# Gated alignment, memory, attention and expert layers on one core: inputs laid out ahead, row jumps scanned once per five steps, key parts split beside the scan and kept in eight places

## The reference

```python
x = x + jnp.tanh(g_xattn[0]) * _L0_xattn_ref(ctx_1024, _layernorm(x, axis=-1))
x = x + jnp.tanh(g_ffn[0]) * _L0_ffn_ref(_layernorm(x, axis=-1), ...)
x = x + jnp.tanh(g_xattn[1]) * _L1_xattn_ref(_layernorm(x, axis=-1), ctx_1024, ctx_1024, ...)
x = x + jnp.tanh(g_ffn[1]) * _L1_ffn_ref(_layernorm(x, axis=-1), ...)

# _L0_xattn_ref, for each batch: small = context (1500), large = x (56)
D = sqrt(max(aa + bb - 2.0 * small @ large.T, 0.0))
R[i, j] = D[i, j] + min(R[i-1, j], R[i, j-1], R[i-1, j-1])
# backtrack from the last corner; of equal ones the diagonal, then i - 1
expanded = zeros((56, 128)).at[j_idx].add(small[i_idx])
# _L1_xattn_ref: 16 heads of 8, keys and values from the context
scores = einsum('bhqd,bhkd->bhqk', Q, K) / sqrt(8)
ctx = einsum('bhqk,bhkd->bhqd', softmax(scores), V)
```

## Time and profile before

| quantity | value |
|---|---|
| device time, median of 3 runs | 730.74 us (726.15 to 734.12) |
| span of the profiled execution | 751.1 us |
| that execution against the median | 20.4 us longer |
| PE, DVE, ACT, POOL busy | 445.6, 444.4, 292.7, 202.9 us |
| data moved | 53.37 MB |

### The profile page before, as it was taken

One profiled execution on the slowest core, in us unless ns is written; L12 is line 12 of the kernel. 1 busy time (PEld: TensorE's weight loads), 2 busy tenths in 40 slices (PEclk: granted clock), 3 DMA queues, 4 the chain that ended last, 5 costly groups with the idle time before them and its releaser, 6 DMA issues.

```text
span 751.1 us, 10182 instructions
## 1 busy us (share of the span) xinstructions
PE 445.6 (59%) x3881; PEld 308.9 (41%) x3881; DVE 444.4 (59%) x1078; ACT 292.7 (39%) x486; POOL 202.9 (27%) x218
## 2 busy tenths in 40 slices
PE   4798211133105787965274105894695695996996
PEld 3798211121003556934172002563463463663443
DVE  5855999998914765455047407783574574815122
ACT  4553332334553457411052000461452452673443
POOL 1221354546253662067706300010101101110000
PEclk9755555556655556986576555896987987996999
DMA  6542000040152431023307999064946857600000
GB/s 164 153 120 72 0 1 0 27 138 33 45 144 86 131 104 62 2 18 95 95 2 92 115 144 120 10 72 54 117 63 71 101 70 79 226 3 1 0 0 14
DMA packets 57825, 53.37 MB, mean 71 GB/s; under 512 B 9456, under 2 KB 48304, under 8 KB 57648
## 3 DMA queue, kind: packets, MB, share of 16 engines
q1 hardware_dynamic: 43152, 39.83, 32.5%
q10 hardware_dynamic: 13088, 9.22, 3.9%
q0 software_dynamic: 1536, 3.67, 1.6%
...
## 4 chain that ended last, share of the span: by engine, by line
PE 39%; DVE 15%; issue 8%; DMA 5%; another core or an unknown queue 3%; ACT 3%; SPq 3%; POOL 1%; ACTq 0%; DVEq 0%; POOLq 0%
PE banks L1568 7%; PE banks L1592 7%; PE banks L1615 5%; PE banks L1471 4%; DVE work L1318 4%; PE banks L1657 3%; PE banks L1665 3%; DMA query_parts<-work 3%; PE banks L1529 3%; DVE mx L1090 2%; SPq L417 2%; DVE arena L1308 2%; PE banks L1432 2%; DMA arena<-query_parts 1%
## 5 line engine op out<-in xcount | busy, mean ns | idle before, releaser
L1090 DVE TENSOR_REDUCE mx<-banks 112x1 f32<-112x500 f32 x192 | 122.7, 674 | 100.2 <-PE banks L1568 99.7
L847 ACT ACTIVATE arena<-banks 128x896 f32<-128x896 f32 x96 | 87.9, 917 | 100.2 <-PE banks L1615 99.4
L1568 PE MATMUL banks<-ctxT,arena 128*112 128x500 bf16 x144 | 63.4, 460 | 59.9 <-DMA arena<-query_parts 36.9
L1432 PE MATMUL banks<-ctxT,Wk_sb 128*128 128x125 f32 (+1 forms) x136 | 56.2, 532 | 29.2 <-ACT work L724 15.7
L1592 PE MATMUL banks<-arena 128*32 128x112 f32 (+1 forms) x1536 | 60.9, 278 | 6.7 <-issue 5.9
L626 POOL TENSOR_TENSOR work<-arena,mk 128x448 f32<-128x448 f32 x7 | 6.5, 932 | 191.5 <-ACT arena L834 191.5
L1568 PEld LDWEIGHTS banks<-ctxT,arena 128*112 128x112 bf16 x144 | 20.8, 145 | 78.1 <-DMA arena<-query_parts 37.1
L1432 PEld LDWEIGHTS banks<-ctxT,Wk_sb 128*128 128x128 f32 x136 | 35.3, 313 | 37.5 <-ACT work L724 20.7
L1424 PE MATMUL banks<-ident,arena 100*128 100x100 f32 x70 | 14.8, 384 | 60.3 <-ACT work L694 57.5
L1615 PE MATMUL banks<-arena,ctxT 128*128 128x112 bf16 (+1 forms) x576 | 44.7, 222 | 6.7 <-issue 6.7
L1615 PEld LDWEIGHTS banks<-arena,ctxT 128*128 128x128 bf16 (+1 forms) x576 | 40.2, 109 | 18.7 <-issue 11.7
...
## 6 DMA issues: line engine op xcount, KB each, us to landing
...
arena<-in_L_ffn_W SPq DMA_DIRECT2D x1, 2048.0 KB, 9.7
...
```

Of the source, the lines that this page charges most:

```text
L847: nc.scalar.activation(Pt[0:rows, g % 2, :].rearrange("p (a n) -> p a n", a=2), banks[0:rows, 2 + 2 * (g % 2):4 + 2 * (g % 2), 0:HQ // 2], ...
L1090: nc.vector.tensor_reduce(mx3[:, b % 2, u // NPIECE, u % NPIECE:u % NPIECE + 1], ps[k % (6 if b == 0 else 2)][0:2 * NJ, 0:PIECE], AX_X, AL ...
L1432: ins = nc.tensor.matmul(ps[KBANKS[n % 7]][:, lo:hi], Wk_sb[:, :], ctxT[:, n * KPIECE + lo:n * KPIECE + hi], start=True, stop=True)
L1568: nc.tensor.matmul(ps[k % ring][0:2 * NJ, 0:PIECE], QP[:, u // NPIECE, b, :], KP[b % 3][:, u // NPIECE, (u % NPIECE) * PIECE:(u % NPIECE + ...
```

## The change

Inputs come laid out by the host: x and the context transposed, the context once more in rows of 100, and one table of weights. The first layer's distances are made in 12 units (3 thirds of 500 context rows, 4 pairs of batches) whose two batches take two halves of PE's columns; the squares are added to them in PSUM by a product with ones, the d2 step of units 6 to 11 stands inside the scan. Jumps are coded by PE per block of five steps (`jump_codes`) and scanned by DVE (`jump_targets`), so that they need neither `hops`, nor the 14 scans, nor the deskew DMAs; the path has 69 hops. Key projection and split move into the scan (`key_step`), with the subtraction of parts done by PE (`take_off`), and the parts wait for their store in eight places. Values are projected between the hops. Query parts are brought to their partitions by products with `picks` instead of through DRAM. Score units are numbered by `DUE`. Key parts of batches 0 and 1 load from the end of the path sums, two DMAs at a time, and each product goes to every sixth partition. The diff, cut:

```diff
+    STORES = 8
+    FIRST_VALUE_HOP = 6
...
-    BESIDE = [3] * 8 + [2] * (NCH * NB)
...
+    KEYS_OF_CHUNK = [0, 1] + 7 * [3] + 5 * [2]
...
+    LEAD = 4
+    DUE = [min(3 * (g + 1), 2 * (g + 1) + LEAD, (NB - 1) * UNITS) for g in range(NB * NCH)]
...
+            sp.dma_start(xT[:, :], x_T[:, :]).then_inc(s_x, 16)
+            for u in range(UN):
+                sp.dma_start(piece(ctxT, u), piece(ctx_T, u)).then_inc(s_ctx[u], 16)
+            sp.dma_start(wts[:, :], weights[:, :]).then_inc(s_w, 16)
+            def store_keys(n):
+                sp.wait_ge(s_kx[2], n + 1)
+                i = n % KPB * KPIECE
+                sp.dma_start(key_parts[n // KPB, :, :, i:i + KPIECE].rearrange("x p i -> p x i"),
+                             kq[n % STORES]).then_inc(s_kd[n % STORES], 16)
...
             def load_key_parts(b):
                 for c, (kx, _) in enumerate(PRODUCTS):
-                    sp.dma_start(KP[b % 3][2 * DH * c:2 * DH * (c + 1), :, :],
+                    if b < 2 and c >= 2:
+                        sp.wait_ge(s_kpl[b][c % 2], 16 * (c // 2))
+                    sp.dma_start(KP[b % 3][c:NPR:len(PRODUCTS), :, :],
                                  key_parts[b, kx].rearrange("(m r) i -> r m i", r=2 * DH)
-                                 ).then_inc(s_kpl[b % 3], 16)
-            for r in range(4):
-                sp.wait_ge(s_kd[r], 16 * NKP // 4)
-            sp.wait_ge(s_vc, NCH // 4 * NB)
-            for t in range(4):
-                sp.wait_ge(s_gath[t], 16 * NHK)
+                                 ).then_inc(s_kpl[b % 3][c % 2], 16)
+            for r in range(STORES):
+                sp.wait_ge(s_kd[r], 16 * len(range(r, NKP, STORES)))
+            sp.wait_ge(s_ex, NB // 2)
             for b in range(2):
                 load_key_parts(b)
-            for part in range(3):
-                sp.wait_ge(s_qs, part + 1)
-                sp.dma_start(query_parts[part], QS[:, part, :]).then_inc(s_qd[part], 16)
-            for c, (_, qx) in sorted(enumerate(PRODUCTS), key=lambda product: product[1][1]):
-                sp.wait_ge(s_qd[qx], 16)
-                sp.dma_start(QP[2 * DH * c:2 * DH * (c + 1), :, :, :].rearrange("r m b n -> r m (b n)"),
-                             query_parts[qx].rearrange("(m r) n -> r m n", r=2 * DH)).then_inc(s_qp, 16)
...
+            def key_step(n):
+                if n < NKP:
+                    act.wait_ge(s_kp, n + 1)
+                    if n >= STORES:
+                        act.wait_ge(s_kd[n % STORES], 16 * (n // STORES))
+                    nc.scalar.activation(kq[n % STORES][:, 0, :], ps[KBANKS[n % KRING]][:, 0:KPIECE], ACT.Identity,
+                                         bias=cols[:, 1:2]).then_inc(s_kx[0], 1)
+                for x in (1, 2):
+                    m = n - x
+                    if 0 <= m < NKP:
+                        act.wait_ge(s_kr[x - 1], m + 1)
+                        nc.scalar.activation(kq[m % STORES][:, x, :], ps[KBANKS[m % KRING]][:, 0:KPIECE], ACT.Identity,
+                                             bias=cols[:, 1:2]).then_inc(s_kx[x], 1)
...
+            def jump_inputs(k):
+                t, n = CODES[k]
+                nc.vector.tensor_tensor(three(left_of(k)), R_slot(t, n, 1, C), R_slot(t, n, 0, C), ALU.is_lt)
+                nc.vector.tensor_tensor(three(rise[k % 2][:, 0:n * C]), R_slot(t + 1, n, 0, C),
+                                        three(mring[:, t % (2 * TB) * C:(t % (2 * TB) + n) * C]), ALU.subtract
+                                        ).then_inc(s_rise, 1)
+            def rows_not_left(k):
+                n = CODES[k][1]
+                ve.wait_ge(s_sgn, k + 1)
+                nc.vector.tensor_tensor(never[k % 2][:, 0:n * C], rises_of(k), left_of(k), ALU.is_lt
+                                        ).then_inc(s_nv, 1)
+            def jump_targets(k):
+                t, n = CODES[k]
+                ve.wait_ge(s_code, k + 1)
+                nc.vector.tensor_tensor_scan(where[:, t * SLOT:(t + n) * SLOT], gate[:, 0:n * SLOT],
+                                             ps[3 - k % 2][:, 0:n * SLOT], 0.0, ALU.add, ALU.max).then_inc(s_carry, 1)
+            D2_AT = {1: (6,), 3: (7,), 5: (8, 9), 7: (10,), 8: (11,)}
...
+            def dots(u):
+                n, g = u // PAIRS, u % PAIRS
+                pe.wait_ge(s_ctx[u], 16)
+                if u < 2:
+                    pe.wait_ge(s_xm, u + 1)
+                else:
+                    pe.wait_ge(s_d2, u - 1)
+                for h in range(2):
+                    nc.tensor.matmul(ps[4 + u % 2][h * J64:(h + 1) * J64, 0:PIECE], xm2[:, 2 * g + h, :],
+                                     piece(ctxT, u)[:, h, :], start=True, stop=False, skip_group_check=True)
+                pe.wait_ge(s_sq, u + 1)
+                for h in range(2):
+                    last = nc.tensor.matmul(ps[4 + u % 2][h * J64:(h + 1) * J64, 0:PIECE], ones[:, 0:J64],
+                                            sqT[:, u % SQ_RING, h, :], start=False, stop=True,
+                                            skip_group_check=True)
                 last.then_inc(s_dot, 1)
+            def turn(u):
+                pe.wait_ge(s_d2, u + 1)
+                if u >= 2:
+                    pe.wait_ge(s_dist, u - 1)
+                for s in range(SPP):
+                    last = nc.tensor.transpose(view(ps[2 + 4 * (u % 2)][0:C, :], [[1, P]], s * P),
+                                               sd[:, u % D_RING, s * C:(s + 1) * C], ident[:, :])
+                last.then_inc(s_turn, 1)
...
+            def take_off(n, x):
+                pe.wait_ge(s_kx[x], n + 1)
+                nc.tensor.matmul(ps[KBANKS[n % KRING]][:, 0:KPIECE], minusb[:, :], kq[n % STORES][:, x, :],
+                                 start=False, stop=(x == 1), skip_group_check=True).then_inc(s_kr[x], 1)
...
+                bank, n = ps[3 - k % 2], CODES[k][1]
+                inner = view(bank, [[SLOT, n], [1, C]], 1)
+                nc.tensor.matmul(bank[:, 0:n * SLOT], one16[:, :], steps16[:, 0:n * SLOT], start=True, stop=False,
+                                 skip_group_check=True)
+                nc.tensor.matmul(inner, one16[:, :], left_of(k), start=False, stop=False,
+                                 skip_group_check=True)
+                nc.tensor.matmul(inner, never16[:, :], never[k % 2][:, 0:n * C], start=False, stop=True,
+                                 skip_group_check=True).then_inc(s_code, 1)
...
+            for k in range(2, NTB):
+                for i in KEY_STEPS[k]:
+                    key_step(i)
+                    if i == KEY_STEPS[k][0]:
+                        jump_codes(k - 2)
+                if k + 2 < NTB:
+                    lane_columns(k + 2)
...
+                due = max(0, h - FIRST_VALUE_HOP + 1) * NB * NCH // (STEPS - 1 - FIRST_VALUE_HOP)
+                for i in range(values, due):
+                    value(i)
...
+                for s in slabs:
+                    for par in range(2):
+                        b = 2 * g + par
+                        last = nc.tensor.matmul(ps[SUM_BANK[g]][64 * par:64 * par + NJ, 0:D],
+                                                Pm[:, g % 2, s, par * NJ:(par + 1) * NJ],
+                                                nat[b][:, s * D:(s + 1) * D],
+                                                start=(s == 0), stop=(s == NS - 1), skip_group_check=True)
...
+            def query_rows(half, m, bank):
+                n0 = half * TOK
+                for x in range(3):
+                    last = nc.tensor.matmul(ps[bank][0:NPR, 0:TOK], picks[:, m, x, :], QS[:, x, n0:n0 + TOK],
+                                            start=(x == 0), stop=(x == 2))
+                last.then_inc(s_ql, 1)
+            pe.wait_ge(s_picks, 1)
+            pe.wait_ge(s_qs, 3)
+            for m in range(NH // 2):
+                query_rows(0, m, m)
...
-                    ahead = UNITS + sum(BESIDE[:g])
-                    units = [divmod(k, UNITS) for k in range(ahead, min(ahead + BESIDE[g], NB * UNITS))]
+                    units = [(1 + k // UNITS, k % UNITS) for k in range(DUE[g - 1] if g else 0, DUE[g])]
```

1027 lines of the change are left out of this document (459 added, 568 removed).

## The result

The changed kernel takes 553.68 us, median of 4 runs (553.44 to 555.59); the kernel before takes 729.95 us over 4 runs. The ratio of the two is 0.761, with a 95% interval of 0.757 to 0.766, so the change takes 24% of the time away. The kernel before has quick executions and others some 10 us longer, and each ratio with an interval in this document compares quick executions alone, so it differs a little from the ratio of the medians (0.759 here). The forecast was 560 with a range of 512 to 612.

The account below looks back on a forecast made before the run. The kernel was taken as a row of stages, each with another engine at its limit. New stage times summed to a span of 570.6 us, taken as 560 us of time; range 540 to 582, with rivals 512 to 612.

Parts of the forecast that it names:

- A: Distances and first ten scan steps: step 10 at 58.4 us instead of 88.7, with 3.05 us a unit.
- R1: Rival: PE stays at half clock up to the end of the scan, giving 597 us; chance 0.12.
- B: Other 60 scan steps: 12 blocks of 4.2 + 3.1, 87.6 us against 85.1; jumps' tail 5.5 instead of 58.2.
- C: Path: 69 hops instead of 55, taken as 62 us against 52.0; 50 or 66 by the period used.
- D: Path sums: instructions in pairs on two column halves, PE below ACT, 27 us instead of 38.5.
- E: Memory layer: value projection leaves the stage, gathers take 40 us, 69 us instead of 94.7.
- R2: Rival: gathers in the memory layer suffer from key loads beside them, +25, 585 us; chance 0.10.
- F: Query parts: the round trip through DRAM goes, 13.5 us instead of 36.8, bounds 9 and 20.
- G: First scores of attention: the second half's 24 matmuls and 8 copies added, 18.4 + 3.6 = 22 us.
- H: Attention: a batch's key load takes 10.7 us under 14.7 of cover, 151 us instead of 204.
- R3: Rival: the strided destination doesn't help; five stalls of 5 us in attention, +25, 585 us; chance 0.10.
- From the span to the time: Profiled span 20.4 us above the median; 570.6 becomes 555, 550 or 571 by where that lies; 560 taken.

Follow-up runs that it names:

- b_same: The kernel before once more with no edit, for a second profile: 730.13 us, with a span of 719.7.
- a_stores4: The changed kernel with four places instead of eight for key parts on their way to DRAM: 562.79 us against 553.13 in the same set.
- a_load_late: The changed kernel with the key-part loads of batches 0 and 1 held back until all gathers have landed: 548.6 us.
- a_weave: The changed kernel with the 16 products of query rows woven between the first score units, all copied by ACT: 543.89 us.
- b_spread: The kernel before with only key parts and query parts going to every sixth partition: 658.95 us against 729.49.
- a_adjacent: The changed kernel with each product's key parts on 16 adjacent partitions again: 587.57 us against 553.68.

## Why the prediction was right

A, the way was right (a gain that comes from feeding PE densely, R1 excluded: granted clock 1.00 from start to step 10, with 0.68 of a unit's 2.51 us spent on transposes) and two sizes were not. The 0.66 that spoke for R1 was in part that execution's own, since up to the first scan step b_same was granted 0.90 and this one 0.69. The transposes of a unit take about 0.7 us and not 1.07 by f32 columns, and nothing is lost in switching between them and the products: a unit is 2.51 us, not 3.05, which is 6.5 of the 8.4 us. No run shows the 3 us for PE's cold start: the clock is at 1.00 from the start on. The sum itself was half a microsecond off (12 + 36.6 + 3 + 1.8 + 4.5 is 57.9, not 58.4). The price of a pair of products, 0.83, was right to 0.09 (1.83 for two pairs), and so was the reason given for it, two column halves side by side: the starts come in pairs.

B, VectorE paces the scan, as forecast, but the term was 11.5 us too large. The operations of a block, by the trace of the changed kernel:

```profile
120.33 0.40 DVE L1162 TENSOR_TENSOR work<-work 128x500 f16<-128x500 f16 x1
...
121.35 0.66 DVE L1153 TENSOR_TENSOR work<-arena 128x500 f16<-128x500 f32 x1
121.92 0.67 DVE L1154 TENSOR_TENSOR work<-arena,work 128x500 f32<-128x500 f32 x1
...
126.05 1.18 DVE L1169 TENSOR_TENSOR_SCAN arena<-work,banks 128x505 f16<-128x505 f32 x1
```

The prices were right: the sum had 0.4, 0.67, 0.67 and 1.19, and the records have 0.40, 0.66, 0.67 and 1.18. What was too large is their sum of 3.1 with gaps. There are no gaps: each starts about 0.1 us before the record of the one ahead ends, so from start to start they add 0.31, 0.57, 0.58 and 1.10 us, 2.56. A part of that falls into the wait between two dependent operations of a step: the next minimum, which needs the scan, starts 0.46 us after it (122.88 to 123.34), an operation that doesn't need it after 0.35 (119.98 to 120.33). A block is 76.1 / 12 = 6.3 us, 4.2 + 2.1. That is the prediction's lower bound, 76, and outside the 7.0 to 7.6 us a block that it named as its sign. The key split was hidden, with the clock at 0.97. That it stays hidden hangs on the eight places. The prediction costed the stores' move at nothing and did not say what fewer places would cost: 9.7 us, by a_stores4.

C, 57.7 against 62, with the last hop at 187.9 us where the prediction's sign had 200 to 225, since A and B were early: the period is 0.72 with one product between hops and about 1.07 with two at half clock; the stage runs between 51 and 58 by the clock it is granted, which the prediction's bounds of 50 and 66 hold. D, 25.4 against 27, right.

E, 71.4 against 69, right in size, and wrong in what it was set against. The step that failed is "between them stands the value projection": its 24 us of waits belonged to one execution. R2 didn't happen: the loads at the spread rate cost the gathers nothing in the 15 to 19 us that they stand beside them. The 2.4 us over the forecast lie between the first index and the last down product, 45.7 us where the sum had 43.3. They are there in a_load_late as well, so they are not the loads', and 1.6 of them are there in b_same (44.9), so the sum was short for the kernel before too; their cause is open.

F and G, 14.7 and 22.3 against 13.5 and 22, right, and a_weave shows that they were not at their bound.

H, 155.3 against 151: the mechanism was right, a load of about 10.7 us under its cover, no wait of PE over 1.1 us, the clock that comes back. b_spread and a_adjacent show it from both sides. The 4.3 us over the sum were not taken apart. R3 was wrong about the partitions and nearly right about the price of the opposite: 34 us, where it had 25 without the clock. The loads run at 215 GB/s where they ran at 117. The Trainium skill ("SBUF — State Buffer", section on Door 1) has the speed of a transfer go by the number of ports that its partitions reach. By its map that number goes from 4 to 13 or 14, an estimate of over three times, and the measured rate went up 1.84 times only. An estimate from the same map by the fullest port, which gets 4 of the 16 partitions before and 2 now, gives twice, as in the prediction, and is the nearer one. Only one stride was run, so that the ports are the reason was not shown.

From the span to the time: the prediction left open whether the 20.4 us lie in the stall or are spread, and took the middle. b_same points to the stall, at 19.3 us of the 20.4. With that the forecast would have been 571, and the error of the stages, 19 us, would have stood in the open. Two errors, 19 us too much in A to I and 13 too little in this step (11 taken off, 2 to be added), cancelled for the most part; a forecast of 560 against 554 is better than its working.
